# The second block's row maxima by VectorE, and four differences of the fourth block's input by GpSimd

## The reference

```python
scale = cond @ norm_w.T + 1.0                       # one row of 512 for each of 4 sequences
ms = jnp.mean(x * x, axis=-1, keepdims=True)
h = x * (scale[:, None, :] * jax.lax.rsqrt(ms + EPS))
val, gate = jnp.split(h @ up_w.T, 2, axis=-1)       # 4096 rows x 512 times 512 x 4096
h = val * jax.nn.gelu(gate, approximate=False)      # 4096 rows x 2048
hq = act_quant(h)      # round(h * 127 / max|row|), clipped, and divided by the same scale
wq = weight_quant(down_w)                           # -1, 0 or 1 times the mean of |down_w|
return hq @ wq.T + x                                # 4096 rows x 512
```

## Time and profile before

| | |
|---|---|
| median of 3 runs | 744.5 us (743.51 to 744.65) |
| the profiled execution | 743.68 us, its span 741.6 us |
| busy in the span | TensorE 733.0 us (99%), VectorE 564.6 (76%), ScalarE 348.9 (47%), GpSimd 102.1 (14%) |
| TensorE's granted clock | full in all slices |

### The profile page before, as it was taken

One profiled execution on the slowest core, in us unless ns is written; L12 is line 12 of the kernel. 1 busy time (PEld: TensorE's weight loads), 2 busy tenths in 40 slices (PEclk: granted clock), 3 DMA queues, 4 the chain that ended last, 5 costly groups with the idle time before them and its releaser, 6 DMA issues.

```text
span 741.6 us, 14381 instructions
## 1 busy us (share of the span) xinstructions
PE 733.0 (99%) x5506; PEld 537.6 (72%) x5506; DVE 564.6 (76%) x1126; ACT 348.9 (47%) x678; POOL 102.1 (14%) x137
## 2 busy tenths in 40 slices
PE   7999999999999999999999999999999999999998
PEld 6544444444688886888778886788878887788854
DVE  5567778998898776888579776888768876587757
ACT  5889766443365533464234642355323443244424
POOL 1211477886230000000000000000000000000000
PEclk9999999999999999999999999999999999999999
DMA  8877683857555454443534345343543334363202
GB/s 331 303 268 231 187 280 118 277 170 251 200 154 157 148 183 124 131 138 106 196 95 157 114 142 160 108 157 101 170 137 103 102 103 134 113 183 102 95 30 85
DMA packets 44564, 117.59 MB, mean 159 GB/s; under 512 B 5584, under 2 KB 5840, under 8 KB 43344
## 3 DMA queue, kind: packets, MB, share of 16 engines
q1 hardware_dynamic: 44496, 116.68, 48.4%
HBM read 99.88 MB, written 16.79 MB: 157 GB/s over the span
## 4 chain that ended last, share of the span: by engine, by line
PE 97%; DMA 1%; DVE 0%; issue 0%; SPq 0%; POOL 0%; ACT 0%; DVEq 0%; POOLq 0%
PE ps_v L589 14%; PE ps_v L591 14%; PE ps_v L590 14%; PE ps_y L717 13%; PE ps_g L589 6%; PE ps_g L591 6%; PE ps_g L590 6%; PE ps_v L607 4%; PE ps_v L608 4%; PE ps_g L608 4%; PE ps_g L607 4%; PE ps_g L609 4%; PE ps_v L609 4%; PE ps_v L796 1%; DMA q<-in_up_t_dram 1%; PE ps_g L796 0%
## 5 line engine op out<-in xcount | busy, mean ns | idle before, releaser
L589 PE MATMUL ps_v<-x_hi,w_hi 128*128 128x256 f16 x968 | 263.9, 273 | 0.1
L591 PE MATMUL ps_v<-x_hi,w_lo 128*128 128x256 f16 x968 | 263.9, 273 | 0.0
L590 PE MATMUL ps_v<-x_lo,w_hi 128*128 128x256 f16 x968 | 263.9, 273 | 0.0
L821 ACT COPY ps_g<-ps_v 128x256 f32<-128x256 f32 x96 | 34.3, 357 | 203.6 <-PE ps_v L591 203.6
L832 ACT ACTIVATE g<-ps_g,w_unscale 128x512 f32<-128x512 f32 x128 | 87.3, 682 | 68.3 <-PE ps_g L591 68.2
L1159 DVE TENSOR_TENSOR ps_v<-ps_v,p 128x256 f32<-128x256 f32 x96 | 41.3, 430 | 94.4 <-PE ps_v L591 94.1
L839 ACT ACTIVATE g<-h 128x512 f32<-128x512 f32 x128 | 81.3, 635 | 62.7 <-DVE h L1171 62.3
L589 PE MATMUL ps_g<-x_hi,w_hi 128*128 128x256 f16 x392 | 106.8, 273 | 0.1
L590 PE MATMUL ps_g<-x_lo,w_hi 128*128 128x256 f16 x392 | 106.8, 273 | 0.0
L591 PE MATMUL ps_g<-x_hi,w_lo 128*128 128x256 f16 x392 | 106.8, 273 | 0.0
L589 PEld LDWEIGHTS ps_v<-x_hi,w_hi 128*128 128x128 f16 x968 | 94.7, 98 | 13.9 <-DVE ps_g L1154 0.3
(11 more groups left out here) (139 smaller groups left out, 937.3 us busy)
## 6 DMA issues: line engine op xcount, KB each, us to landing
w_lo<-w_lo_dram SPq DMA_DIRECT2D x96, 448.0 KB, 3.3
q<-in_up_t_dram SPq DMA_DIRECT2D x16, 512.0 KB, 4.7
xt<-in_x_cols_dram SPq DMA_DIRECT2D x8, 1024.0 KB, 4.9
res<-in_x_rows_dram SPq DMA_DIRECT2D x26, 256.0 KB, 3.6
out_dram<-res SPq DMA_DIRECT2D x26, 256.0 KB, 2.7
xs<-in_x_rows_dram SPq DMA_DIRECT2D x22, 256.0 KB, 3.6
w_lo_dram<-w_lo SPq DMA_DIRECT2D x16, 256.0 KB, 4.5
dw<-in_down_t_dram SPq DMA_DIRECT2D x8, 512.0 KB, 6.5
```

Source lines behind the costliest of these rows:

```text
L589: pe.matmul(to, w_hi[:, wh:wh + P], hi, start=start and kt == 0, stop=False, skip_group_check=True)
L590: pe.matmul(to, w_hi[:, wh:wh + P], lo, start=False, stop=False, skip_group_check=True)
L591: last = pe.matmul(to, w_lo[:, wl:wl + P], hi, start=False, stop=(kt == 1), skip_group_check=True)
```

## The change

The second block (b = 1) takes the way of `turn_peaks` and `spread_peaks` in place of `turn_max`, `row_scales` and `spread_scale`; its `row_dequant` is four instructions in place of one. The four differences for the input of c = 3 are made by GpSimd, once its last `sum_weights` is done, with the same waits. ScalarE's highs of that input are placed in passes 34 (XB11, XT1), 36 (XT2), 37 (XT3), 38 (XB21, XB22) and 39 (XN4), where they stood in passes 34 and 35. VectorE's low of XB11 and of XT1 stay in pass 34, the others in pass 47.

```diff
-    V_FIRST = 2
+    V_FIRST = 1
...
-                    if j == (2 if b < 3 else 5):
+                    if j == (2 if b < 2 else 4 if b < 3 else 5):
                         high(b + 1, XT2)
-                    if j == (2 if b < 3 else 8):
+                    if j == (2 if b < 2 else 5 if b < 3 else 8):
                         high(b + 1, XT3)
-                    if j == (3 if b < 3 else 9):
+                    if j == (3 if b < 2 else 6 if b < 3 else 9):
                         high(b + 1, XB21)
                         high(b + 1, XB22)
-                    if j == (3 if b < 3 else 11):
+                    if j == (3 if b < 2 else 7 if b < 3 else 11):
                         high(b + 1, XN4)
...
             for k in range(J):
                 sum_weights(k)
+            c, before = 3, 4
+            pool.wait_ge(xn_ready, c * KT + 2)
+            pool.wait_ge(peak_step, (c - 2 - V_FIRST) * PEAK_STEPS + 1)
+            pool.tensor_tensor(ta[:], xt[:, 0:2, HB:TB], xt[:, 0:2, 0:HB], ALU.subtract).then_inc(t_ready, 1)
+            pool.wait_ge(xn_ready, c * KT + 4)
+            pool.wait_ge(t_ready, before + 1)
+            pool.wait_ge(scale_rows, c - 1)
+            pool.tensor_tensor(tb[:], xt[:, 2:4, HB:TB], ta[:], ALU.subtract).then_inc(t_ready, 1)
+            pool.wait_ge(t_ready, before + 2)
+            pool.tensor_tensor(xt[:, 0:2, HB:TB], xt[:, 2:4, HB:TB], xt[:, 0:2, HB:TB],
+                               ALU.subtract).then_inc(t_ready, 1)
+            pool.wait_ge(x_lo_ready, made_at(c, XT1))
+            pool.tensor_tensor(ta[:], xt[:, 2:4, 0:HB], tb[:], ALU.subtract).then_inc(t_ready, 1)
...
                 if 1 <= b < NB - 1:
-                    if j == 2:
+                    if j == 2 and b != 2:
                         difference(b + 1, XT1)
                     if j == (2 if b < 3 else 4):
-                        difference(b + 1, XT2)
+                        if b != 2:
+                            difference(b + 1, XT2)
                         low(b + 1, XB11)
                     if j == (2 if b < 3 else 7):
-                        difference(b + 1, XT3)
+                        if b != 2:
+                            difference(b + 1, XT3)
                         low(b + 1, XT1)
-                    if j == (2 if b < 3 else 10):
+                    if j == (2 if b < 3 else 10) and b != 2:
                         difference(b + 1, XN4)
```

## The result

| | before | after |
|---|---|---|
| median | 744.0 us (22 runs, 743.23 to 746.57) | 745.84 us (22 runs, 744.53 to 747.39) |
| ratio | | 1.0021 (95% interval 1.0014 to 1.0028) |
| span of the profiled execution | 741.6 us | 744.5 us |
| TensorE from its first product of pass 33 to its first of pass 48 | 194.19 to 274.42: 80.23 us | 195.59 to 277.29: 81.70 us |

The change makes the kernel slower by 0.21%, 1.6 us of 744.0 (1.0 to 2.1), which is the 0.2% that I took as the bound of what can be told; the two medians by themselves lie 1.84 us apart. The forecast was +0.9 us, in words "no change"; 745.84 lies in the range, which reaches from 743.7 to 747.0 and holds every case but the ceiling and the worst of rival 2.

The account below looks back on a forecast made before the run. TensorE bounds the kernel, sharing the bound with VectorE in passes 33 to 35. A 0.9 us later seed_gate(35), TensorE's saved 0.90 counted, plus 0.05 for row_dequant gave +0.9 us, 745.4 on the median's scale; range 743.7 to 747.0.

Parts of the forecast that it names:

- the ceiling: TensorE, passes 33 to 36: at most 1.08 us gained, 0.90 of removed products plus the 0.18 stop.
- rival 2: Passes 34 and 35: the shared port holds VectorE longer, the spread ends at 213.4; 747.0 us, +0.33%, chance 0.17.
- XT1 was priced at 1.25: GpSimd's first difference, 128x512 f32, behind the last weight sum: 1.25 us, from 210.55 to 211.8.
- The second hold: Pass 34: low(3, XT1) on VectorE comes behind GpSimd's XT2, running 213.5 to 214.05.
- the contention inside the spread: VectorE's spread_peaks(1) beside GpSimd's last sum: two or three pieces pay 0.4 us each, ending at 211.3.
- XT1's hold against the next operation, the low of XB11: Pass 34: low(3, XB11), issued at 211.3, waits for XT1's end and ends at 212.4.
- The 0.25 for the running maximum: VectorE: peak_of(33) falls beside GpSimd's difference XN4 and pays some 0.25 us.
- the forecast's case (+0.3 to +1.5): Whole kernel: slower by +0.3 to +1.5 us around the forecast +0.9, chance 0.56.
- `row_dequant(1)` in pass 37: VectorE: four instructions, 0.97 us for 0.22; after the rest before pass 38, costs TensorE 0.05 (0 to 0.2).
- Rival 1 (even): VectorE's stretch in passes 34 and 35 comes out even: -0.3 us, 744.2 on the median's scale, chance 0.17.
- Rival 3: GpSimd's last sum gets its data later than 207.33; one microsecond more gives +1.9, 746.4; chance 0.07 beyond +1.5.

Follow-up runs that it names:

- vector_later: Kernel before, with second-block maxima on VectorE and its four differences and two lows spread over passes 39 to 44, no GpSimd: ratio 0.9977, stretch -1.05 us.
- low_xt1_later: Changed kernel with the low of XT1 moved from pass 34 to 40, the last high to 42: ratio 1.0000 to the kernel before, stretch -0.22 us.
- both_mended: Changed kernel with GpSimd's XT1 behind the spread scales, both lows in passes 40 and 41, last high in 43: ratio 0.9996 to the kernel before.
- differences_only: Changed kernel with second-block maxima back on TensorE, GpSimd still making the four differences behind its sums: ratio 1.0004 to the kernel before, stretch +1.32 us.
- maxima_only: Kernel before with only the second block's maxima moved to VectorE, all differences still on VectorE in pass 34: ratio 1.0033, stretch +3.58 us.
- xt1_after_scales: Changed kernel with one wait moved, so GpSimd's XT1 also waits for the spread scales: ratio 1.0027 to the kernel before, stretch +3.06 us.

## Why the prediction was right in its direction and short in its size

- The bound and the ceiling held. TensorE's queue lost 0.90 us, the stop before `third(35)` was VectorE's, and the most that could be had was 1.08: vector_later got 1.05 in its trace.
- XT1 was priced at 1.25 and took 1.26, and it waited behind the sum as said. Both came earlier than I had them: the sum at 206.75 and not 207.33, XT1 at 209.86 and not 210.55, just ahead of the spread's last copies.
- The second hold was right: the low of XT1 "comes behind" XT2, 1.06 more than alone. low_xt1_later shows its worth. Of the two stops, each forecast at about 1.0, the one before `third(35)` was 0.93 and the one before `fourth(34)` 1.56.
- **The mis-sized term was the contention inside the spread.** I had it end at 211.3, with some 0.9 of contention; it took 2.09, and ended at 213.71 - 1.40 = 212.31. I gave the sum's operations 0.9 (measured 1.07) and let the last three copies slip through before XT1; they were held for 1.02. I had counted XT1's hold against the next operation, the low of XB11, as some 0.5, which then went free. So `hidden(33)` is 1.31 later and not 0.68, `seed_gate(35)` 1.43 and not 0.9 (216.77 against 219.60 - 1.40 = 218.20). The 0.25 for the running maximum was too much: it took 0.80 for 0.68.
- On my own bound the result stands on the line: the trace's +1.47 is just inside the forecast's case (+0.3 to +1.5), the runs' +1.6 just outside it. The chance of 0.25 for slower by over 0.2% and of 0.72 for the same describe it less well than an even split would have. The second rival's picture, XT1 holding up the rest of the spread, was half of the truth: 212.3 lies between the forecast's 211.3 and its 213.4.
- `row_dequant(1)` in pass 37, its remaining highs and the lows of pass 47: no more than 0.05, as said. The stretch is 0.04 longer than the delay at `third(35)`.
- Rival 1 (even) fell for this order and is what one gets when one low is moved. Rival 3 is no effect of the change, but a spread between executions: the last sum began at 206.62 to 208.05 on one scale.
- The Trainium skill (SBUF — State Buffer, Who interferes with whom) calls the shared port an exclusive lock held for a whole instruction. The traces agree, with numbers: 1.58 for three copies that take 0.56, 1.53 for a running maximum of 0.68 (both_mended), and 0.69 for the low of XB11 where GpSimd was itself waiting. The same section says that a reduction never takes part, and here the spread's reduction kept its 0.25 while GpSimd's last sum ran.

## What to carry to other kernels

When a second engine takes over work that shares a port with the first, count what it holds up among the instructions that stay, for its longest operation and at every place where both work, and above all among chains of small dependent ones: three copies of 16 columns lost more than a microsecond to one difference. And look first for passes in which the loaded engine rests: the same six operations, moved 5 to 10 passes later and left on VectorE, gave, in its trace, the whole ceiling that no division between the engines in the full pass reached. An instruction that waits for another engine belongs where nothing urgent is queued behind it, as the one low of 0.69 us shows.

## What the runs showed of the hardware

- A GpSimd difference of 128x512 f32 takes 1.26 to 1.28 us undisturbed and 1.59 to 1.68 when VectorE's lows stand against it; of 128x8 0.20. Four of them run one behind the other in 1.35 to 1.42 each (differences_only, both_mended).
- VectorE's operation pays nearly the whole of GpSimd's remainder and not a share of it: 1.75 for 0.69 beside XT2.
- TensorE's granted clock fell to 0.50 for 3.1 to 3.3 us behind two stops with 0.6 us of products between them (2.37 and 0.51 in maxima_only, 1.16 and 1.07 in xt1_after_scales), with products 0.213 apart in place of 0.109, and this cost 1.7 to 1.8 us. Behind the stops of the changed kernel (1.56 and 0.93, with 2.0 us between) it stayed at 1.00.
- VectorE's turning of h_max, 128x512, in squares (0.70) and its reductions (0.69, 0.25) took no longer beside GpSimd; two-operand work in SBUF, copies and scalings did.
- The start of pass 33 moves by 1.5 us between executions (194.0 to 195.6) for kernels that are alike up to it, so spans of single executions can't be compared at this size; a stretch between two landmarks can.
